# Second layer of a two-layer transformer kernel: routing work moved into gaps, register loads split, and the last sums shared by ScalarE and VectorE

## The reference

```python
xn = _layernorm(x, axis=-1)
x = x + _L0_attn_ref(xn, ...) + _L0_ffn_ref(xn, ...)
xn = _layernorm(x, axis=-1)
x = x + _L1_attn_ref(xn, ...) + _L1_ffn_ref(xn, ...)
# L1_attn: no softmax; norms over the tokens
q, k, v = jnp.split(x @ W + b, 3, axis=-1)
kv = jnp.sum(k / jnp.linalg.norm(k, axis=1, keepdims=True) * v, axis=1, keepdims=True)
return q / jnp.linalg.norm(q, axis=1, keepdims=True) * kv
# L1_ffn: 16 experts of width 128, 4 per token, and a shared expert of width 512
probs = jax.nn.softmax(xt @ w_router, axis=-1)
top_w, top_i = jax.lax.top_k(probs, 4)
top_w = top_w / jnp.sum(top_w, axis=-1, keepdims=True)
g = silu(xt @ we1[e]) * (xt @ we3[e])
shared = silu(xt @ ws1) * (xt @ ws3) @ ws2
out = shared / 5 + moe_out * (4 / 5)
```

## Time and profile before

| | |
|---|---|
| median of 3 runs | 937.84 us (937.28 to 938.01) |
| the profiled execution | 937.78 us, its span 936.0 us |
| mean granted clock of PE | 0.959 |
| busy: PE, DVE, ACT, POOL | 851.0, 646.8, 428.7, 433.8 us |
| HBM read, written | 60.30, 45.96 MB |

### The profile page before, as it was taken

How to read it: one execution, slowest core, us unless ns; L and a number is a source line. 1 busy time by engine, 2 the same in 40 slices (tenths; PEclk the granted TensorE clock), 3 DMA queues, 4 the chain that set the end, 5 groups by cost and what they waited for, 6 DMA issues and landing times. The chain is left out here.

```text
span 936.0 us, 16088 instructions
## 1 busy us (share of the span) xinstructions
PE 851.0 (91%) x4769; PEld 456.2 (49%) x4770; DVE 646.8 (69%) x1542; ACT 428.7 (46%) x758; POOL 433.8 (46%) x720
## 2 busy tenths in 40 slices
PE   5988789899999999999999987796999889999995
PEld 3533223334444444444444321375744467778885
DVE  5589799888788888888887872376452734444558
ACT  2633145465666566665666667455111133333300
POOL 3322064514643436534354464205777147777810
PEclk9998598999999999999999989997899999999998
DMA  9644952201451112712111122381432035545474
GB/s 329 203 145 121 226 108 79 91 19 35 105 99 36 58 36 65 129 51 64 35 46 30 46 69 63 96 321 64 147 120 96 28 113 155 153 152 163 136 308 165
DMA packets 61731, 105.42 MB, mean 113 GB/s; under 512 B 12118, under 2 KB 45398, under 8 KB 60886
## 3 DMA queue, kind: packets, MB, share of 16 engines
q1 hardware_dynamic: 41110, 49.57, 19.5%
q0 software_dynamic: 16000, 45.70, 14.5%
q10 hardware_dynamic: 4544, 9.21, 3.2%
HBM read 60.30 MB, written 45.96 MB: 114 GB/s over the span
## 5 line engine op out<-in xcount | busy, mean ns | idle before, releaser
L1143 DVE TENSOR_REDUCE part_max<-ps_row 128x1 f32<-128x512 f32 (+3 forms) x560 | 353.7, 671 | 69.4 <-PE ps_row L1297 40.8
L1013 ACT ACTIVATE probs<-ps_st 128x1024 f32<-128x1024 f32 (+3 forms) x320 | 278.4, 896 | 204.6 <-PE ps_st L1276 203.4
L1201 PE MATMUL ps_o<-probs,v_all 128*17 128x512 f32 (+3 forms) x1280 | 149.9, 540 | 14.2 <-ACT probs L1013 8.9
L1297 PE MATMUL ps_row<-ks,qs 96*128 96x512 bf16 (+3 forms) x320 | 110.3, 379 | 12.9 <-DVE part_max L1143 9.9
L1297 PE MATMUL ps_row<-xt_ks,qs 96*128 96x512 bf16 (+3 forms) x320 | 103.1, 350 | 1.0 <-DVE part_max L1143 0.5
L1536 POOL DMA_INDIRECT yd<-moe_ys,moe_home x79 | 82.5, 1045 | 29.8 <-POOL moe_home L1530 16.2
L1276 PE MATMUL ps_st<-qs,ks 99*128 99x512 bf16 (+3 forms) x320 | 88.4, 358 | 3.6 <-DMA qs<-max_parts 3.5
L1276 PE MATMUL ps_st<-qs,xt_ks 99*128 99x512 bf16 (+3 forms) x320 | 83.9, 352 | 2.1 <-ACT probs L1013 1.3
L1566 PE MATMUL moe_ps_h<-w,moe_xs_t 128*128 x316 | 83.0, 386 | 0.0
L1297 PEld LDWEIGHTS ps_row<-ks,qs 96*128 96x128 bf16 x320 | 32.0, 100 | 95.3 <-DVE part_max L1143 56.8
L1487 DVE TENSOR_TENSOR moe_hid<-moe_ps_h,moe_act 128x128 f32<-128x128 f32 x79 | 23.1, 292 | 75.3 <-ACT moe_act L1470 75.3
(11 more groups left out here) (287 smaller groups left out, 1331.9 us busy)
## 6 DMA issues: line engine op xcount, KB each, us to landing
moe_xs<-xd SPq DMA_DIRECT2D x79, 129.0 KB
qk_parts<-probs SPq DMA_DIRECT2D x16, 384.0 KB, 3.3
qs<-qk_parts SPq DMA_DIRECT2D x96, 64.0 KB, 2.5
moe_xs<-xd POOLq DMA_DIRECT2D x47, 128.0 KB, 2.4
yd<-moe_ys POOLq DMA_DIRECT2D x47, 128.0 KB, 2.1
xd<-zeros POOLq DMA_DIRECT2D x2, 2048.0 KB, 15.5
moe_w<-in_w ACTq DMA_DIRECT2D x2, 2048.0 KB
w<-in_we SPq DMA_DIRECT2D x1, 4096.0 KB, 20.3
```

What stands on the lines that cost most here:

```text
L1013: act.activation(probs[:, at % NPB, :, off:CH], ps_st[at % 2][:, :, off:CH], ACT.Exp, scale=HD ** -0.5).then_inc(exp_done, 1)
L1143: dve.tensor_reduce(part_max[reduced % 2][:, h:h + k, i, j:j + 1], bank[:, 0:k * w].rearrange("p (h w) -> p h w", h=k), AX_X, ALU.max).the ...
L1201: mm = pe.matmul(ps_o[32 * q:32 * q + HD + 1, off:CH], m.v_all[:, k, g * HG + q, :], probs[:, (at + q // 2) % NPB, q % 2, off:CH], start=F ...
L1297: mm = pe.matmul(cols, qs[c][0:KROWS, h, i * P:(i + 1) * P], ks[g % 2][0:KROWS, h, j * CH:j * CH + w], start=True, stop=(j < c))
```

## The change

In `stage_second` the turns go two tiles at a time and the scores one pass later, behind the output matmuls of passes 9 to 17. The scores and choices of chunk 1 move from inside the loop to behind the last norm, the first slots from pass 14 to 16. The rest is put between parts of the gram product. Each chunk has its own PSUM columns for logits, ranks and counts. The norm arithmetic is cut into pieces that stand between `gated` units 0 to 9, and `bq` is added in four quarters. In `stage_experts` PE loads one expert number per tile and three per body, and waits already implied are dropped. In the last part ACT multiplies the home rows in place, and DVE adds two tiles per instruction.

```diff
@@ stage_experts, scalar
+            for n in range(T // 2):
+                act.wait_ge(fetched[n], 32)
+                for k in range(top):
+                    for i in (2 * n, 2 * n + 1):
+                        mul = act.activation(yg[i][:, k, :], yg[i][:, k, :], ACT.Copy, scale=m.r["weight"][:, i, k:k + 1])
+                    mul.then_inc(scaled, 1)
@@ stage_experts, vector
-                pair = (2 * n, 2 * n + 1)
-                dve.wait_ge(fetched[n], 32)
+                both = m.x[:, 2 * n:2 * n + 2, :]
                 for k in range(top):
-                    for i in pair:
-                        step(dve.scalar_tensor_tensor(m.x[:, i, :], yg[i][:, k, :], m.r["weight"][:, i, k:k + 1],
-                                                      m.x[:, i, :], ALU.mult, ALU.add))
-                    step.sync()
+                    dve.wait_ge(scaled, n * top + k + 1)
+                    step.then(dve.tensor_tensor(both, yg_pair[n][:, :, k, :], both, ALU.add))
@@ stage_experts, tensor
-                    m.r["tile_e"][0:1, bass.ds(j + (EPAD - U), U + BODY)], engines=[mybir.EngineType.PE], min_val=0,
+            def experts_of(j, n):
+                return nc.values_load_multi_w_load_instructions(
+                    m.r["tile_e"][0:1, bass.ds(j + EPAD, n)], engines=[mybir.EngineType.PE], min_val=0,
...
+            def load_late(j):
+                for n, e in enumerate(experts_of(j - 3, 3)):
+                    experts[n - 3] = e
...
+                    experts[u] = experts_of(j, 1)[0]
...
-                    if since(j, 2):
-                        pe.wait_ge(x_copied, j - 1)
...
-            rolled(pe, 3, tiles, BODY, tick, load_experts)
+            rolled(pe, 3, tiles, BODY, tick, load_late)
@@ stage_second, scalar
-                if i > TC and i % TC == 3 and i < T:
-                    act.wait_ge(shift_ready, i // TC)
-                    for t in range(TC):
-                        normalize((i // TC - 1) * TC + t)
-                if i in (11, 15):
-                    exp_of(i // TC - 2)
-                if i >= 2 * TC and i % TC == 0:
-                    copy_turned(i // TC - 2, range(TC))
+                if i >= 7 and i % TC == 3:
+                    act.wait_ge(shift_ready, i // TC)
+                    normalize(i - 7)
+                    normalize(i - 6)
+                if i >= 8 and i % TC == 0:
+                    normalize(i - 6)
+                    normalize(i - 5)
+                    copy_turned(i // TC - 2, range(2))
+                if i >= 5 and i % TC == 1:
+                    root_of(i // TC - 1)
+                if i >= 9 and i % TC == 1:
+                    copy_turned(i // TC - 2, range(2, TC))
+                if i == 12:
+                    exp_of(0)
@@ stage_second, vector
-                if i in (11, 15):
-                    scores_of(i // TC - 2)
-                if i in (13, 17):
-                    best_of(i // TC - 3)
-                if i == 14:
+                if i == 12:
+                    scores_of(0)
+                if i == 13:
+                    best_of(0)
+                if i == 16:
                     chunk_slots(dve, step, r, 0, ranks_ready, slots_ready)
...
+            gated(5)
+            squares()
+            gated(6)
+            key_values()
+            gated(7)
+            inverse_norms()
+            gated(8)
+            key_values_over_norms()
+            gated(9)
+            weighted()
...
-            step.then(dve.tensor_tensor(m.x[:, :, :], m.x[:, :, :], bq[:, :].unsqueeze(1).to_broadcast([P, T, D]),
-                                        ALU.add))
+                moved(4 * (n - 12), 4 * (n - 11))
```

More of the change, by code:

```diff
@@ L1410, in stage_experts @@
         tail_done, finished = l.sem("moe1_tail_done"), l.sem("moe1_finished")
+        scaled = l.sem("moe1_scaled")
+        yg_pair = [yg8[:, 2 * n:2 * n + 2, :, :] for n in range(T // 4)] + [
+            spare4[:, 2 * n:2 * n + 2, :, :] for n in range(T // 8)] + [last4[:, 2 * n:2 * n + 2, :, :] for n in range(T // 8)]
         step_sem = l.sem("moe1_dve")
@@ new lines, in _, with squares @@
+            bqk, bk, bv = bias[:, 0:2 * D], bias[:, D:2 * D], bias[:, 2 * D:3 * D]
+            def squares():
+                dve.wait_ge(norms_done, 1)
+                step.then(dve.tensor_scalar(t1[:, :], bqk, float(S), None, ALU.mult))
+                step.then(dve.scalar_tensor_tensor(t1[:, :], ps_sums[:, :], 2.0, t1[:, :], ALU.mult, ALU.add))
+                step.then(dve.tensor_tensor(t1[:, :], t1[:, :], bqk, ALU.mult))
+                dve.tensor_tensor(square[:, :], ps_ones[:, :], t1[:, :], ALU.add).then_inc(square_ready, 1)
@@ L1889, in _, with moved @@
+            def moved(first, last):
+                step.then(dve.tensor_tensor(m.x[:, first:last, :], m.x[:, first:last, :],
+                                            bq[:, :].unsqueeze(1).to_broadcast([P, last - first, D]), ALU.add))
             gated(0)
+            sums_of()
             gated(1)
+            products()
+            gated(2)
             choice_weights(dve, step, r, TOP1, TOP1 / (TOP1 + 1))
             tables = tile_tables(dve, step, r, NT1)
-            for n in range(2, BEFORE_NORMS):
+            next(tables)
@@ L1894, in _ @@
+            for n in (3, 4):
+                gated(n)
+                next(tables)
+            gated(5)
[8 more added lines that the diff above has]
+            weighted()
+            for n in (10, 11):
+                gated(n)
                 next(tables, None)
+            for n in range(12, 16):
                 gated(n)
-            dve.wait_ge(gram_copied, KH)
@@ L1931, in _ @@
-            step.then(dve.tensor_tensor(t2[:, :], t2[:, :], t1[:, 0:D], ALU.mult))
-            step.then(dve.tensor_tensor(kv[:, :], kv[:, :], t2[:, :], ALU.mult))
-            step(dve.tensor_tensor(bq[:, :], bias[:, 0:D], kv[:, :], ALU.mult))
-            step.then(dve.tensor_scalar(t2[:, :], kv[:, :], float(TOP1 + 1), None, ALU.mult))
-            step(dve.tensor_tensor(wq[:, :, :], w[:, :, 0:D], t2[:, :].unsqueeze(1).to_broadcast([P, KH, D]), ALU.mult))
-            step.sync()
-            for n in range(BEFORE_NORMS, len(units)):
-                gated(n)
@@ L1950, in _, with turn @@
         def _(pe):
-            def turn_and_score(c):
-                pe.wait_ge(xn_ready, c * TC + (TC if c < C - 1 else 1))
-                for i in range(c * TC, (c + 1) * TC):
+            def turn(tiles):
+                for i in tiles:
+                    pe.wait_ge(xn_ready, min(i, T - TC) + 1)
                     if i >= 2:
@@ L2050, in _ @@
             mm.then_inc(norms_done, 1)
-            shared(BEFORE_NORMS)
-            pe.wait_ge(norms_read, 1)
-            pe.wait_ge(square_ready, 1)
-            for n in range(BEFORE_NORMS + 1, len(units)):
+            for n in range(4, len(units)):
                 shared(n)
+            pe.wait_ge(wq_ready, 1)
             pe.wait_ge(m.tail_in, 16)
```

208 lines of the change are left out of this document (116 added, 92 removed).

## The result

| | before | after |
|---|---|---|
| median of the runs | 937.56 us (935.16 to 938.01, 4 runs) | 924.0 us (922.4 to 925.04, 4 runs) |
| ratio | | 0.9859, 95% interval 0.9836 to 0.9882 |
| profiled execution: time, span | 937.78, 936.0 us | 922.4, 920.6 us |

The change makes the kernel 13.6 us faster. The forecast was 914.6 us with a range of 908.0 to 923.5, so the sign was right, the gain was forecast 70% too large, and the result lies half a microsecond outside the range.

A forecast was written before the change was run, and what follows sets the result against it. The prediction took TensorE as near full almost everywhere and VectorE as binding the last stage. It summed 937.8 - 14.8 (second stage) - 3.9 (expert numbers) - 4.5 (last stage) = 914.6 us, range 908 to 923.5.

The forecast's parts named there:

- The stage's end: End of the second stage, before the experts: 734.6 us instead of 749.4, -14.8 us.
- Rival 3: Second stage: the scatter binds, first slots at 643 us, POOL ends the stage at 736.9, total 917 us; chance 0.15.
- The scatters' start and length: POOL in the second stage: first slots at 640 us, last scatter issued at 731.5 instead of 729.53, landed at 733.9.
- The shared expert's start: Second stage: reordered loop and routing start the shared expert at 661.5 us instead of 673.46, -12.0 us.
- The first wait stays: Routing: PE's wait for DVE's first choices, followed by half clock from 632 to 638 us, was to remain.
- The norms between the units: Shared expert: norm pieces placed between units remove PE's three waits, -4.3 us.
- Expert numbers: Expert loop: three register values loaded per batch and one per tile, -3.9 us.
- The bet on single loads: Expert loop: single-value loads taken in the lower half, up to 0.26 us, costing tiles nothing.
- the one at the batch starts: Expert loop: 0.2 us of loss left at each batch start.
- Rival 1: Expert loop: loads per tile stall PE; mild 926 us, chance 0.14, or strong 945.4 us, chance 0.04.
- The last sums: Last stage: DVE takes 29.2 us instead of 33.7 with ACT multiplying, -4.5 us.
- Rival 2: Last stage: ACT becomes the last bound at 0.52 us a multiply, total 920 us; chance 0.12.

The follow-up runs named there:

- the control: The changed kernel itself run again, unedited, on an undisturbed chip: 924.32 us, ratio 0.9871 to the kernel before.
- e5: The changed kernel with POOL writing the next pair's tags between two scatters, on a chip with standstills: ratio 0.9593 to the kernel before.
- e10: The changed kernel with best_of(2) and best_of(3) ahead of slots, first slots in VectorE's gap, exp_of(0) ahead of norms: 919.78 us, ratio 0.9815.
- e12: The changed kernel with SyncE instead of POOL waiting for the landed scatters, in the experts' stage: 921.67 us, ratio 0.9843.
- e15: e10 without the change of the masks' order, on a chip with standstills: ratio 0.9913 to the kernel before.
- e8: The changed kernel with seven unused matmuls where PE waits for the experts, on a chip with standstills: ratio 0.974 to the kernel before.
- e11: e10 with three and three unused matmuls where PE waits for the experts: 920.06 us, ratio 0.984 to the kernel before.
- e13: e17 with nine and three unused matmuls in PE's wait for the experts, on a chip with standstills: ratio 0.9966 to the kernel before.
- e18: e17 with nine and three unused matmuls, on another chip with standstills than e13: ratio 0.9835 to the kernel before.
- e17: e10 with e12's edit, no unused matmuls, on a chip with standstills: ratio 0.9912 to the kernel before.
- e7: e5 with masks first, the first chunk's slots in VectorE's gap and exp_of(0) ahead of two norms: ratio 0.9544 to the kernel before.
- e1: The kernel before with the changed second stage alone, on a chip with standstills: ratio 0.9792, about -20 us.

## Why the prediction was wrong, point by point

**The stage's end, -14.8 forecast, -7.4 us in the profiled run and -5.6 in the control (both counted to the first expert tile).** This is the step that failed. It compared two paths, PE and DVE at 734.6 and POOL "landed" at 733.9, and let the stage end with the later one. POOL's path does not end with the landing: its drain of 5.3 us follows, which by my own numbers would have put the end at 739.2, or 919.2 us in all. Counted from the stage's first matmul, POOL was to have landed at 133.3 us; it had at 136.2 (734.6, the branch behind its wait), 2.9 later, and the drain adds 5.3. The row was in the old trace, and I had not looked at what the barrier's line does, since POOL was hidden then. e5, e10 and e12 show that this path sets the end. Rival 3 named the right engine and the right sign in the profile (PE idle for 7 us), but priced it without the drain at 917.

**The scatters' start and length.** I took the first slots at 640.0, 2 us later than before; counted alike they came 3.3 us later in the profiled run and 4.2 in the control. The handovers of rival 3 were real. The chain of scatters also grew, from 92.3 us in the one trace of the kernel before to 93.6 and 94.5 us. One edit that I costed at nothing has a part in it, the addition of `bq` in four pieces. Before, it was one piece behind POOL's last scatter; now the pieces fall into the chain (DVE and POOL timelines of the changed kernel, then of e10):

```profile
727.36 1.22 DVE L1948 TENSOR_TENSOR x_res<-x_res,bq 128x1024 f32<-128x1024 f32 x1
727.74 1.68 POOL L1719 DMA_INDIRECT xd<-xn,slot  x1 [0.30 <-issue]
...
722.92 1.22 DVE L1948 TENSOR_TENSOR x_res<-x_res,bq 128x1024 f32<-128x1024 f32 x1
722.30 0.97 POOL L1719 DMA_INDIRECT xd<-xn,slot  x1 [0.30 <-issue]
723.27 0.91 POOL L1717 CAST xn<-home 128x2 f32<-128x2 int32 x1
```

The POOL operation that begins while a piece runs is the one that gets longer. In the changed kernel that is a scatter, 1.63 to 1.69 us instead of 0.97, three times; in e10 and e12 it is the cast behind a scatter, 0.91 to 0.95 us instead of 0.19, three times, while the scatter that had begun before the piece keeps its 0.97. Either way it costs 2.1 to 2.2 us in all. The net growth is smaller, because the kernel before had two scatters of 2.18 and 2.03 us beside DVE's operations on `masks` and the changed kernel has one, of 2.09: all 64 took 64.4 us before and 65.4 after, the casts 7.0 and 7.9. e10's earlier start was partly eaten by its casts (9.4 us together) and the waits ahead of them (2.7 instead of 1.3); its chain took 96.3. In e15, where DVE stood still, no scatter took over 1.01 us and the chain 88.5. That coincidence in time is what I can show; no run moved the pieces alone. The Trainium skill, "SBUF — State Buffer", section "SBUF: two separate sides", says that VectorE operations with two SBUF inputs and GpSimd operations that read SBUF exclude each other through a shared pair of ports, each for a whole instruction. These rows agree with it for GpSimd's side. The other side does not show: pieces of the changed kernel and of e10 that began while a scatter ran took 1.21 to 1.22 us, as those of e15 behind the last scatter did.

**The shared expert's start, -12.0 forecast, -5.2 us measured** (72.8 to 67.6, counted alike). The last norm came 4.9 us earlier instead of 7.0, and then the way to the first unit took 22.1 us where I had 17.5. The path from the last norm to the first unit is hardly shorter than before (22.4 us). The timelines of DVE and PE have the pieces:

```profile
645.75 0.22 DVE L1839 TENSOR_REDUCE peak<-scores 128x4 f32<-128x64 f32 x1 [1.20 <-ACT scores L1735]
...
651.65 0.23 DVE L262 COPY given<-ps_l 128x64 f32<-128x64 f32 x1 [2.35 <-PE ps_l L242]
...
657.08 0.20 PE L241 MATMUL ps_ab<-any,before 128*128 128x64 bf16 x1 [0.99 <-DVE any L254]
...
662.79 0.20 PE L241 MATMUL ps_ab<-any,before 128*128 128x64 bf16 x1 [2.79 <-DVE any L254]
...
662.86 3.35 PE L2014 MATMUL ps_gram<-xn 128*128 128x257 f32 x8
```

I had DVE's work back to back. It waits 3.55 us in two places, first for an exponential that stands on ACT behind two copies and a table load of 1.28 us, which I had left out, then for ranks that PE issues in its written order behind gram matmuls. The last eight records of gram (four matmuls) take 3.35 us instead of 1.8, at a granted clock of 0.58 from 662.8 to 666 us, behind the wait of 2.79 us.

For the late norm the clock is the likeliest cause. "The first wait stays", I wrote of the half clock behind the first choices. Windows view, changed kernel:

```profile
630.40:642.80 12.40, 11.88 (x37) 9.50 (x38) 8.37 (x36) 4.31 (x12) 2.38 (x4) 0.50 0.04 13
```

Here PE waits 2.82 us for DVE behind the first choices (the kernel before had no wait for them; its longest one there, 1.09 us, was for a copy of ACT) and then runs at 0.50 for 12.4 us instead of 7.0 (631 to 638 us). DVE waits 1.24 and 1.76 us for output products in that time. No run tested this alone.

With the masks first (e10) the first unit came at 59.6 us, 8 earlier still. It bought nothing at the stage's end, for the reason above.

**The norms between the units.** Right: all three waits of the earlier trace rows for norms are gone, and only the 0.97 us for the last hidden tile stands.

**Expert numbers, -3.9 forecast, -1.5 us measured.** The bet on single loads held, the one at the batch starts did not. Loads of one and of three values, by line, and PE's waits in the loop:

```profile
L1552 PEldq TENSOR_LOAD <-tile_e x80: 296/302/932, 740.4 to 876.8; - x80
...
PE moe_ps_x L1566 <- issue: 2.7, 4, 1.0
```

A single value takes 0.30 us, above my limit of 0.26, yet the tiles in a batch still stand 1.63 us apart, so the lead is longer there, as I had argued. The five loads of three take 0.77 to 0.93 us, and the first single one 0.30 or more behind it: the four batch starts lose 0.28 to 0.97 us each, 2.7 in all, where I had 0.2 each. The line through 8 and 20 values would have given 0.2 us for three. The floor of about 600 ns under a `tensor_load` that the Trainium skill gives ("DMA: Bandwidth & Descriptors", section "Latency and other measured facts") does not hold here: the median of these loads, 302 ns, is half of it. Rival 1 did not come, in either strength.

**The loop's start at half clock.** Not in the forecast, and no part of the loss. It costs about 2.3 us (e8, e11), but the kernel before pays it as well, and a longer idle time ahead of it did not make it dearer (the counts are with e8). The granted clock was 0.67 from 753.1 to 758.2 us before and 0.57 from 743.4 to 749.5 after.

**The last sums, -4.5 forecast, -4.6 us measured.** Right in its parts. DVE and ACT timelines:

```profile
889.88 0.69 DVE L1519 TENSOR_TENSOR x_res<-moe_yg,x_res 128x512 f32<-128x512 f32 x1 [10.04 <-ACT moe_yg L1484]
890.74 5.49 DVE L1519 TENSOR_TENSOR x_res<-moe_yg,x_res 128x512 f32<-128x512 f32 x7 [0.17 <-ACT moe_yg L1484]
...
900.47 2.86 DVE L1519 TENSOR_TENSOR x_res<-moe_yg,x_res 128x512 f32<-128x512 f32 x4
...
888.94 6.50 ACT L1484 ACTIVATE moe_yg<-moe_yg,weight 128x256 f32<-128x256 f32 x16 [11.45 <-DMA moe_yg<-yd]
```

DVE's additions come 0.72 apart, it runs for 29.1 us from ACT's first multiply on (888.94 to 918.05; forecast 29.2), and ACT takes 0.41 us a multiply (forecast 0.42). Rival 2 is out.

**The sum.** By parts, with the mean of the two executions of the changed kernel for the second stage: -6.5 - 1.5 - 4.6 = -12.6 us, against 13.6 measured first and 12.8 in the control. Of the 23.2 us forecast, 8.3 were lost at the stage's end and 2.4 in the expert loop, of which 1.9 stand at the batch starts (2.7 us of waits instead of 0.8). The range was too narrow on the upper side because its rivals were each priced alone, and the drain in none of them.

## What to carry over

A stage ends when every engine's queue reaches the barrier, so when work off the critical path is about to become the bound, follow it to the barrier's own line, with its drain, and not only to its last landing. An engine that gets 7 us ahead gains nothing once another is last (e10); and what is issued beside that other engine has a price even if its own engine is idle. Matmuls put into a wait to hold the clock shortened the loop by 2.4 and 2.7 us (e8, e11) and by 0.5 and 0.7 (e13, e18 against e17), but late or long ones cost as much: in e11 they started behind 8.3 us of rest and ran at half clock themselves, in e13 and e18 they held up the barrier. No version with them was faster as a whole.

## What the runs showed of the hardware that I had not expected

- POOL's drain at the end of a block with 64 scatters took 5296 ns in the kernel before, in the change and in e10, 5386 in e5 and 5387 in e7; it counts from its last instruction, not from the landing (e12).
- On four of the five chips of the experiments, engines other than POOL stood still for up to 53 us (ACT in e18) while the scatters ran. The trace names nothing on the core as the releaser; it has "remote" there. ACT and DVE in e15, and POOL's last scatter:

```profile
710.95 0.65 ACT L1774 COPY gram<-ps_gram 128x257 f32<-128x257 f32 x2 [48.37 <-remote]
722.49 0.60 ACT L1782 ACTIVATE gate<-ps_t 128x512 f32<-128x512 f32 x1 [9.59 <-remote]
...
727.59 0.69 DVE L1893 TENSOR_TENSOR o_t<-ps_t,gate 128x512 f32<-128x512 f32 x1 [35.38 <-remote]
...
722.40 0.96 POOL L1719 DMA_INDIRECT xd<-xn,slot  x1 [0.30 <-issue]
```

  The kernel before took 961 to 997 us there instead of 937. The changed second stage alone (e1) gave 20 us on such a chip. What holds the engines up was not tried and stays open.
